# The base of the output formed by ScalarE, with its store on ScalarE's queue, in a fused decoder layer

## What is computed

```
def _layernorm(x, axis=-1, eps=1e-05):
    m = jnp.mean(x, axis=axis, keepdims=True)
    v = jnp.var(x, axis=axis, keepdims=True)
    return (x - m) / jnp.sqrt(v + eps)
...
x = x + _L0_attn_ref(_layernorm(x), Wq, Wk, Wv, Wff, bff)              # 16 heads
x = x + _L0_xattn_ref(ctx_1024, ctx_1024, _layernorm(x), ...)          # 750 context rows
x = x + _L0_ffn_ref(_layernorm(x), ...)                                # look-up of 8 values per row
...
# in _L0_ffn_ref, with hidden_states = _layernorm(x):
    top_scores, top_idx = jax.lax.top_k(scores, K)                     # K = 8 of N = 2048 keys
    w = jax.nn.softmax(top_scores, axis=-1)
    v = aux_values[top_idx]
    agg = jnp.einsum('bsk,bskh->bsh', w, v)
    out = hidden_states + gate[..., None] * agg
```

## Time and profile before

| | us |
|---|---|
| median of 3 runs | 2780.71 (2779.53 to 2780.83) |
| the profiled execution, its own time | 2788.23 |
| its span in the profile | 2786.2 |
| TensorE matmuls busy | 2556.4 (92% of the span) |
| VectorE busy | 2146.0 (77%) |
| ScalarE busy | 1431.3 (51%) |
| GpSimd busy | 683.1 (25%) |

### The profile page before, as it was taken

The page is one execution under the profiler, slowest core; times in us unless marked ns, Lnnn a source line. Parts: engine busy times, 40 slices in busy tenths (PEclk is TensorE's granted clock), DMA queues, the critical chain, the costliest instruction groups (busy, mean ns, idle before and its releaser), DMA issues.

```text
span 2786.2 us, 56938 instructions
## 1 busy us (share of the span) xinstructions
PE 2556.4 (92%) x19090; PEld 2104.0 (76%) x19090; DVE 2146.0 (77%) x4207; ACT 1431.3 (51%) x4247; POOL 683.1 (25%) x650
## 2 busy tenths in 40 slices
PE   6899999999999999999999999999999999999730
PEld 4578878887888788878887888778888887788520
DVE  5456888888888888888888888888888888887552
ACT  2345554555555545555555455555554555555252
POOL 0001222222222222222222222222222222222254
PEclk9899999999999999999999999999999999999955
DMA  5223354454544444444444445444445454444799
GB/s 189 53 80 80 107 132 121 128 137 130 133 121 112 130 125 123 138 131 131 128 111 128 131 113 138 131 131 131 115 126 134 106 139 130 132 130 111 202 205 178
DMA packets 131542, 358.87 MB, mean 129 GB/s; under 512 B 21906, under 2 KB 26514, under 8 KB 123267
## 3 DMA queue, kind: packets, MB, share of 16 engines
q0 software_dynamic: 63520, 160.60, 24.4%
q1 hardware_dynamic: 63188, 192.15, 23.6%
q10 hardware_dynamic: 4784, 5.46, 0.6%
HBM read 316.37 MB, written 41.78 MB: 129 GB/s over the span
## 4 chain that ended last, share of the span: by engine, by line
PE 74%; DVE 8%; ACT 7%; issue 7%; DMA 2%; POOL 1%; DVEq 0%; ACTq 0%; POOLq 0%; SPq 0%
PE psX L1144 43%; PE psA L1144 13%; PE psA L1153 5%; PE psF L1144 4%; PE psA L1210 4%; DVE top L999 3%; PE psA L1233 2%; ACT paT L640 2%; PE psX L1153 2%; ACT sc L640 1%; DMA vg<-in_L_ffn_aux_values,idx 1%; ACT xT_hi L663 1%; DVE xmax L948 1%; PE psF L1153 1%; DVE idx L1002 1%
## 5 line engine op out<-in xcount | busy, mean ns | idle before, releaser
L589 POOL DMA_INDIRECT vg<-in_L_ffn_aux_values,idx x512 | 491.7, 960 | 1550.5 <-DVE agg L1028 1053.8
L684 ACT ACTIVATE pa<-psA,nmax 112x224 f32<-112x224 f32 x1024 | 444.6, 450 | 197.8 <-DVE nmax L917 194.5
L917 DVE TENSOR_REDUCE nmax<-psA 112x4 f32<-112x896 f32 x256 | 267.1, 1085 | 100.9 <-PE psA L1210 100.9
L1144 PE MATMUL psX<-big,gT 128*112 128x375 f32 x1024 | 333.4, 478 | 0.6 <-ACT gT L711 0.6
L1028 DVE SCALAR_TENSOR_TENSOR agg<-vg,wt,agg 112x512 f32<-112x512 f32 x406 | 303.8, 748 | 9.2
L1144 PE MATMUL psX<-pT,cx 125*128 125x224 f32 x1536 | 299.1, 355 | 0.0
L1144 PEld LDWEIGHTS psX<-pT,cx 125*128 125x128 f32 x1536 | 288.0, 190 | 4.0 <-issue 0.3
L932 DVE TENSOR_TENSOR pa<-pa,rsum 112x896 f32<-112x896 f32 x256 | 279.4, 1091 | 8.8
L1144 PEld LDWEIGHTS psX<-big,gT 128*112 128x112 f32 x1024 | 175.2, 176 | 126.0 <-issue 0.9
L1153 PE MATMUL psA<-ident,pa 112*112 112x112 f32 x2048 | 227.2, 262 | 19.5 <-DVE oT_lo L895 19.4
L640 ACT COPY paT<-psA 112x448 f32<-112x448 f32 x512 | 237.2, 560 | 11.4 <-PE psA L1153 9.4
(11 more groups left out here) (220 smaller groups left out, 5957.0 us busy)
## 6 DMA issues: line engine op xcount, KB each, us to landing
big<-in_ctx_t SPq DMA_DIRECT2D x32, 1500.0 KB, 8.1
cx<-in_ctx SPq DMA_DIRECT2D x32, 1344.0 KB
xa<-in_x SPq DMA_DIRECT2D x64, 224.0 KB
centered<-in_x_t SPq DMA_DIRECT2D x32, 448.0 KB, 4.6
x<-in_L_attn_bff POOLq DMA_DIRECT2D x32, 448.0 KB, 5.7
x<-cb_scratch POOLq DMA_DIRECT2D x32, 448.0 KB, 5.9
x<-in_x SPq DMA_DIRECT2D x31, 448.0 KB
out<-x SPq DMA_DIRECT2D x30, 448.0 KB, 3.1
```

The source lines that it names most:

```text
L589: pool.indirect_dma_start(vg[:, c % SLOTS, k, :], None, aux_values, bass.IndirectOffsetOnAxis(ap=idx[:, t, n:n + 1], axis=0))\
L684: last = nc.scalar.activation(pa[:, t, h, :], psA[0:R, h, t * S:(t + 1) * S], ACT.Exp, bias=nmax[:, k % 2, h, t:t + 1], accum_out=rsum[:, ...
L917: nc.vector.tensor_reduce(nmax[:, k % 2, h:h + 2, :], psA[0:R, h:h + 2, 0:T * S].rearrange("p h (t s) -> p h t s", t=T), AX_X, ALU.max, ne ...
L1144: last = nc.tensor.matmul(dst, stationary, moving, start=n == 0, stop=n == len(pairs) - 1)
```

## The change

ScalarE forms the base, SyncE and GpSimd have no part in it any more. With m the mean and r the 1/sqrt of a row, x2 + (x2 - m) r = x2 (1 + r) - m r. VectorE forms the two numbers of each row, `grow` = 1 + r and `shift` = -m r, with two small instructions right behind the norm. ScalarE waits for them (`base_formed`), runs one instruction for each of the two tiles with `grow` as scale and `shift` as bias, waits for its own result (`base_ready`) and issues the store itself. The buffer, the place in the order and the later waits for `base_ready` and `base_stored` stay.

```diff
@@ semaphores and small tiles
+        grow, shift = sb("grow", [R, T]), sb("shift", [R, T])
+        base_formed = sem("base_formed")
@@ SyncE
-            def store_base(b, _):
-                if isinstance(b, int) and b >= WHOLE:
-                    return
-                sp.wait_ge(base_ready, b + 1)
-                sp.dma_start(tiles(row(out, b)), x2[:, :, :]).then_inc(base_stored, 16)
...
-                          ("F", "norm"): store_base,
@@ GpSimd
-            def add_base(b, _):
-                pool.wait_ge(x2_normed, b + 1)
-                dst = x2
-                if isinstance(b, int) and b >= WHOLE:
-                    dst = base[b]
-                    wait_full(pool, "A", FILL["A", "mix", NB - 1], B - 1)
-                nc.gpsimd.tensor_tensor(dst[:, :, :], x2[:, :, :], xnf[:, :, :], ALU.add).then_inc(base_ready, 1)
@@ ScalarE
+            def add_base(b, _):
+                dst = x2
+                if isinstance(b, int) and b >= WHOLE:
+                    dst = base[b]
+                    wait_full(act, "A", FILL["A", "mix", NB - 1], B - 1)
+                act.wait_ge(base_formed, b + 1)
+                for t in range(T):
+                    last = nc.scalar.activation(dst[:, t, :], x2[:, t, :], ACT.Identity, scale=grow[:, t:t + 1], bias=shift[:, t:t + 1])
+                last.then_inc(base_ready, 1)
+                if not (isinstance(b, int) and b >= WHOLE):
+                    act.wait_ge(base_ready, b + 1)
+                    act.dma_start(tiles(row(out, b)), x2[:, :, :]).then_inc(base_stored, 16)
...
+                           ("F", "norm"): add_base, ("F", "turn"): turn("F", "turn", xnfT), ...
@@ VectorE, in f_norm behind norm("F", ...)
+                nc.vector.scalar_tensor_tensor(shift[:, :], mv["F"][:, :, 0], -1.0, rstd["F"][:, :], ALU.mult, ALU.mult)
+                nc.vector.tensor_scalar(grow[:, :], rstd["F"][:, :], 1.0, None, ALU.add).then_inc(base_formed, 1)
```

More of the change, by code:

```diff
@@ L610, in _ @@
             pool.wait_ge(small_loaded, 16 * SMALL)
-            pipeline(pool, {("Z", "scale"): add_scaled,  ("R", "bias"): bias_x, ("X", "norm"): bias_x1, ("F", "norm"): add_base,
+            pipeline(pool, {("Z", "scale"): add_scaled,  ("R", "bias"): bias_x, ("X", "norm"): bias_x1,
                             ("G", "sum"): next_gather, ("F", "top"): first_gather})
@@ L807, in _ @@
                            ("X", "score"): x_exp, ("X", "prob"): x_probs_turned, ("X", "mix"): x_mixed,
-                           ("F", "turn"): turn("F", "turn", xnfT), ("F", "route"): route, ("F", "score"): f_score,
+                           ("F", "norm"): add_base, ("F", "turn"): turn("F", "turn", xnfT), ("F", "route"): route, ("F", "score"): f_score,
                            ("F", "top"): f_top})
```

## The result

| | us |
|---|---|
| before, median of 9 runs | 2780.83 (2779.53 to 2784.29) |
| changed, median of 9 runs | 2788.96 (2787.07 to 2791.51) |
| ratio | 1.0027, interval 1.0018 to 1.0035 |
| iteration before, norm of batch 1 to norm of batch 29, by 28 | 79.385 |
| iteration changed | 79.583 |

The change costs 8.1 us. The prediction was 14.9 us slower (2795.6), in a range of 2781 to 2810: the direction and the mechanism were right, and the size was about half.

A forecast was written before the change was run, and what follows sets the result against it. The prediction took TensorE's chain, fed by ScalarE's `gT`, as the bound, not GpSimd's addition. 30 iterations x 0.48 us + 0.5 at the end = 14.9 us on 2780.71 gave 2795.6 us, range 2781 to 2810.

The forecast's parts named there:

- The terms on ScalarE and VectorE: From the second norm to `gT`: base instructions 1.51 us, self-wait and issue 0.54, four `gT` instructions 1.49; VectorE 0.1 to 0.3 later.
- the example iteration: The loop iteration around 1342 us, from which the prediction read its times and TensorE's delay.
- wait for itself: On ScalarE between the base and the store issue: 0.17 us, ahead of 0.37 for the issue.
- 0.48 us late per iteration: TensorE's 16 matmuls behind `gT` would end at 1351.63 instead of 1351.15 us, delaying the chain by 0.48.
- the room: How much later `gT` may end before TensorE's 16 matmuls end later: 0.42 us.
- The time from `gT` to the matmuls: From the end of `gT` to TensorE's first matmul, read from batch 31: 2615.04 to 2615.29 us.
- The factor 30: The delay was counted for 30 iterations, F of batches 0 to 29.
- the signs that the prediction named: In the changed profile: line 709 at 0.80 us, issue 0.35, `gT` row 1.49, TensorE idle 0.5, iteration 79.9, line 891 0.16.
- The end: In batch 31 the Ln at line 780 starts later, its table load behind the base instructions: 0.5 us.
- Hidden after all: Rival, chance 0.19: `gT` on ScalarE ends under about 1345.8 us, so no delay; time 2781 to 2786 us.
- A slow issue: Rival, chance 0.13: the DMA issue on ScalarE takes 1.2 us, matmuls 1.3 late per iteration; time 2820 us.
- GpSimd's hold on VectorE: Rival, chance 0.06: 0.44 us at line 891 comes back if VectorE has no idle time ahead of line 917; 2767 us.

The follow-up runs named there:

- e2: The change, but SyncE issues the store as before while ScalarE still forms the base; ratio to the kernel before 1.0004.
- e3: The change, but ScalarE issues the store behind the four `gT` instructions of the same iteration; ratio to the kernel before 0.9997.
- e4: The change plus one unused 112x256 ScalarE instruction ahead of the two that form the base, batches 0 to 29; ratio to the kernel before 1.0061.
- e6: The kernel before, with GpSimd still adding, but ScalarE issuing the store where the change has it; ratio to the kernel before 1.0114.
- e1: The kernel before, unedited, run again for a second profile and more times; ratio 1.0002, iteration 79.403 us.
- e7: The kernel before plus three unused statistics on VectorE ahead of the copy at line 891; ratio to the kernel before 1.0035.
- e9: The kernel before plus three unused statistics on VectorE behind the copy at line 891; ratio to the kernel before 1.0078.
- e10: e3 plus three unused statistics on VectorE behind the copy at line 891; ratio to the kernel before 1.0029.
- e5: The change, unedited, measured again on another chip; ratio to the kernel before 1.0025.
- e12: The change, unedited, measured once more on a third chip; ratio to the kernel before 1.0029.

## Why the prediction was right in its mechanism and off in its size

**What bounds the kernel: right.** GpSimd's addition was on nobody's path, and its removal gave the loop nothing (e2, e3). The `gT` instructions are what ScalarE's new work delays.

**The terms on ScalarE and VectorE: right.** `base_formed` was forecast 1.17 us after the start of the norm; `grow` ends at 1.15. VectorE's later work was to move by 0.1 to 0.3 us and moved by 0.02, so that VectorE's idle time was not needed as a cover. One base instruction takes 0.807 us (0.80 forecast from three rows, none of which had the form), the two 1.52 (1.51), self-wait, issue and restart 0.61 (0.61), the four `gT` instructions 1.46 (1.49). In the example iteration `gT` ends at 4.77 us after the start of the norm, forecast 4.82. The Trainium skill, page "ScalarE: Activation LUTs", section "What ACT_TABLE_LOAD costs", gives 186 ns plus 0.833 ns a column plus about 93 ns for each operand that is a pointer. That is an estimate of 0.80 us, and the trace agrees with 0.807.

The 0.61 us is worth a closer look, because only part of it is the wait and the issue. Line 713 of the changed kernel (minimum, median and maximum, ns), and ScalarE in batch 28, which lies behind the loop in the part written out:

```profile
L713 ACTq DMA_DIRECT2D out<-x x30: 323/324/357, 230.1 to 2537.9; - x30
L713 ACTq FUSED_REGOPS  x27: 46/51/51, 309.6 to 2378.9; - x27
L713 ACTq MOVE out<-x x27: 29/29/29, 309.6 to 2379.0; - x27
...
2456.78 1.52 ACT L709 ACTIVATE x<-x,shift,grow 112x512 f32<-112x512 f32 x2 [3.04 <-DVE grow L882]
2458.33 0.33 ACTq L713 DMA_DIRECT2D out<-x  x1
2458.72 1.47 ACT L698 ACTIVATE gT<-psX,gb 128x224 f32<-128x224 f32 x4 [0.41 <-ACT x L709]
```

Two register instructions stand ahead of the issue in the 27 batches of the loop (1 to 27), and in none of the three stored outside it (0, 28 and 29). In the loop the first of them starts 0.03 us after the base is complete and the issue 0.17 us after it; in batch 28 the issue itself starts after 0.03. A third one stands behind the issue. So 0.20 of the 0.61 us is register work of the loop, and outside it the same step takes 0.41. The prediction took its 0.17 from SyncE's issue, which has the same two register instructions ahead of it; the number was right for the loop, its name ("wait for itself") was not.

**The step that failed** is the term "0.48 us late per iteration" of TensorE, which measured 0.20; behind it stands the room, booked at 0.42 us and in fact 0.57. In the change `gT` ends 0.78 us later than before in the mean (4.78 against 4.00) and 0.20 of it is felt; in e4 it ends 1.26 us later and 0.69 is felt. Both leave 0.57 to 0.58. Three things made the term too large:

- *The time from `gT` to the matmuls, 0.15 us.* I took it from batch 31, where 0.25 us lie between the end of `gT` and the first matmul. In the loop of the changed kernel it is 0.10 (1346.38 to 1346.48), and in e4 and e6 0.10 to 0.11. In the changed kernel batch 31 has its 0.25 again, and e4 has 0.25 in the iterations written out on either side of the loop. The trace shows what differs. In the loop one semaphore instruction on TensorE waits for `gT`, ends 0.04 us after it, and the first weight load starts at 0.07. In the written-out iterations two semaphore instructions run one after the other, from 0.04 to 0.20 us after the end of `gT`, and the load starts at 0.22. The 5.27 us for the matmuls was right.
- *The example iteration, 0.09 us.* TensorE does not stand at the same place against VectorE in each iteration. Of before, one iteration later than the earlier trace rows:

```profile
1420.44 1.00 DVE L857 TENSOR_SCALAR nx<-x,mv_F,rstd_F 112x512 f32<-112x512 f32 x2
...
1424.66 1.09 DVE L917 TENSOR_REDUCE nmax<-psA 112x4 f32<-112x896 f32 x1 [0.75 <-PE psA L1210]
```

  Here VectorE's maxima, which wait for TensorE's scores, start 4.22 us after the start of the norm, in the example 4.04. Over the loop the scores start 3.01 to 3.27 us behind the norm, in the mean 3.10; the example had 3.02. Before, the product behind the 16 matmuls moves with them: it starts 9.41 to 9.44 us after the norm in 17 of the 27 loop iterations and 9.59 to 9.66 in the other 10. But the base hangs on VectorE, and in the changed kernel that product starts at 9.69 to 9.74 wherever the scores lie. So an iteration loses 0.25 to 0.29 us or about 0.10, and the one that I took was among those with the greatest loss.
- *The end of `gT`, 0.05 us* earlier than forecast.

Together 0.29, which leaves 0.48 - 0.29 = 0.19 per iteration, against the 0.20 read.

The factor 30 was too large as well. In batches 0, 28 and 29, written out, `gT` ends at 4.58 to 4.60 us, by the 0.20 of register work sooner, and the product behind starts where it did before (9.66 to 9.67): these three lose nothing.

Of the signs that the prediction named, the base instructions, the issue, the single `gT` row and line 891 came as said. The iteration is 79.58 and not 79.9, and TensorE's idle time is 0.25 us of "issue" and not 0.5 put down to ScalarE. The sign of being wrong "`gT` ending before the score's first weight load" was badly chosen: that load needs `gT`, so it follows it in every version.

**The end: right where it could be seen.** The Ln of line 780 starts 4.08 us behind the start of the last norm, 3.48 before: 0.6 us later (0.5 forecast), behind the table load that moved:

```profile
2669.26 1.52 ACT L709 ACTIVATE x<-x,shift,grow 112x512 f32<-112x512 f32 x2 [11.90 <-DVE grow L882]
2670.79 1.28 ACT L780 ACT_TABLE_LOAD   x1
2672.09 0.26 ACT L780 ACTIVATE var_all<-var_all 112x64 f32<-112x64 f32 x1
```

From the last norm to the end, however, it takes 119.1 us with the change and 119.2 in e1, and from the norm of batch 29 252.0 and 253.3, so that this delay does not reach the end in these two executions.

**The sum.** 27 x 0.205 = 5.5 us in the loop, as read from the 28 iterations (5.5 us over the first profile of before, 5.0 over e1) and within the interval of the measured ratio (5.0 to 9.7 us). The medians differ by 8.1, 8.1 and 8.4 us in the three comparisons. The 2.6 us that the loop leaves lie outside it or are noise; between the last norm and the end the profiled executions of before, the change, e1, e2 and e3 take 117.7 to 122.5 us, the kernel before alone 119.2 and 122.5, and I could not place the 2.6 us. The cause shown here accounts for the loop alone.

**The rivals.** *Hidden after all* failed, but was nearer than its 0.19 said: a `gT` 0.2 us sooner would have hidden it, as batches 0, 28 and 29 show in the changed kernel itself, and e2 and e3 with `gT` at 4.07. *A slow issue* did not occur: the 30 issues took 0.323 to 0.357 us. *GpSimd's hold on VectorE* had its condition right. The Trainium skill, page "SBUF — State Buffer", section "SBUF: two separate sides", says that of a GpSimd operation and a VectorE operation that needs the shared ports the one which starts first holds them for its whole instruction, and the other blocks. The copy at 0.60 beside the addition, 0.17 without it in the change, e3 and e7, agrees, and e9 against e10 shows both what it is worth and the condition: VectorE must have no idle time behind it.

No version is clearly faster than the kernel before. The change with the store behind `gT` is as fast as the kernel before (0.9997 and 1.0010).

## What to carry to other kernels

Before work is moved to an engine that is half idle, write down for that engine what stands directly behind the new place, when it was last ready in time, and who waits for it: here the room was 0.57 us on an engine with about half of its time idle. A wait for one's own result and a DMA issue right behind it cost the engine their full time (0.61 us in the loop, 0.20 of it register work); with the four useful instructions between them they cost nothing. Whether the register work could be done ahead of the wait, which would leave 0.41 us and by batches 0, 28 and 29 no loss, was not tested. And a room of a few tenths is not read from one iteration: take it as the mean over the loop, and a latency from the loop too, not from the part written out. Count the factor from the iterations that really have the wait.

## What was not expected of the hardware

- The same step costs different times in the loop and in the iterations written out around it. From the end of `gT` to the first matmul that waits for it: 0.10 us in the loop (the change, e4, e6), 0.25 outside (before, the change, e4), where two semaphore instructions run behind the end of `gT` instead of the end of one. From ScalarE's result to its next instruction, by way of the DMA issue: 0.61 us in the loop and 0.41 outside, with three register instructions fewer.
- The program took 1% longer on the two chips of e5 to e12 (2812.5 and 2807.9 against 2780.8 and 2784.3 us), at the same granted clock (0.97). In the loop of e12 about 0.6 us more of idle time than in the first profile of the change appears on VectorE ahead of the maxima (line 919) at two of the four places in an iteration. The profile puts it down to TensorE's scores, but those are done as early as before. From ScalarE's instruction at line 745 to the second maxima it takes 7.09 us in the first profile of the change, and in the mean 8.13 in e5 and 7.80 in e12. The ratios of the change are the same on all of them. Open.
